# GNN plus top-2 mixture of experts on one core: translations of blocks into items moved behind the last runs, batch loads ahead of them

## The reference, cut to what matters

```python
x = x + gnn(layernorm(x), src, dst, edge_weight, W, b)
x = x + ffn(layernorm(x), gate_w, gate_b, W1, b1, W2, b2)

def gnn(f, src, dst, w, W, b):                 # 12500 nodes, 256 features, 212500 edges, dst sorted
    agg = segment_sum(f[src] * w[:, None], dst)
    return einsum('ni,oi->no', agg, W) + b

def ffn(x, ...):                               # 8 experts, 256 -> 512 -> 256
    probs = softmax(x @ gate_w + gate_b)
    top2_vals, top2_idx = top_k(probs, 2)      # each node goes to two experts
    out = sum over experts e of  cw[:, e] * (gelu(x @ W1[e] + b1[e]) @ W2[e] + b2[e])
```

## The kernel before, in words

| turn | items whose loads are issued | tiles translated | runs sent | batch (tiles) |
|---|---|---|---|---|
| 208 | 179, 180 | 72-75 | 92, 93 | |
| 209 | 181, 182 | 76-79 | 94, 95 | |
| 210 | 183, 184 | 80-83 | | 0 (48-51) |
| 211 | 185-187 | | 96, 97, then the tails | 1 (52, 53) |
| 212 | 188-190 | | | 2 (54-57) |
| 213 to 221 | three in each turn, to 216 | | | 3 to 9 in turns 213 to 219 |

## Time and profile before

### The profile page before, as it was taken

The page is one execution under the profiler, slowest core; times in us unless marked ns, Lnnn a source line. Parts: engine busy times, 40 slices in busy tenths (PEclk is TensorE's granted clock), DMA queues, the critical chain, the costliest instruction groups (busy, mean ns, idle before and its releaser), DMA issues.

```text
span 2566.9 us, 46927 instructions
## 1 busy us (share of the span) xinstructions
PE 2069.9 (81%) x11178; PEld 1625.8 (63%) x11179; DVE 1591.4 (62%) x6566; ACT 653.7 (25%) x1900; POOL 1802.5 (70%) x1909
## 2 busy tenths in 40 slices
PE   4666786688899889888897899896978878886595
PEld 2444564477677677765775678674757666765485
DVE  7888546446565465465666756776776656776344
ACT  3332111122222122221321223221223222232131
POOL 7665777777777777777767767577777777752473
PEclk8776888899999999998999999998989889998797
DMA  8766755867868879778788699597889788795696
GB/s 285 250 206 211 233 176 167 258 217 250 292 215 272 262 222 293 255 233 271 221 263 274 200 302 299 171 307 251 272 275 315 230 272 281 262 284 199 221 370 227
DMA packets 304350, 646.04 MB, mean 252 GB/s; under 512 B 62536, under 2 KB 197226, under 8 KB 291402
## 3 DMA queue, kind: packets, MB, share of 16 engines
q1 hardware_dynamic: 145320, 325.55, 37.4%
q0 software_dynamic: 90384, 248.17, 32.2%
q10 hardware_dynamic: 68370, 69.23, 7.7%
HBM read 543.70 MB, written 208.20 MB: 293 GB/s over the span
## 4 chain that ended last, share of the span: by engine, by line
POOL 26%; PE 19%; DVE 18%; issue 14%; DMA 11%; SPq 11%; ACT 1%; DVEq 1%; ACTq 0%; POOLq 0%
POOL rows L523 22%; SPq L504 8%; PE bank L885 7%; DMA slots<-stage 5%; PE bank L978 5%; PE bank L962 4%; DMA stage<-sorted_x 3%; POOL got L564 2%; DVE spread L1366 2%; DVE bn L1345 2%; SPq L454 1%; PE bank L905 1%; DVE pre_bn L1322 1%; DVE square_n L1413 1%; POOL rows L564 1%
## 5 line engine op out<-in xcount | busy, mean ns | idle before, releaser
L523 POOL DMA_INDIRECT rows<-xhat,src_t x1488 | 1423.0, 956 | 500.8 <-issue 446.2
L885 PE MATMUL bank<-rows,spread 128*80 128x256 f32 x3328 | 870.4, 421 | 163.4 <-DMA rows<-xhat,src_t 70.8
L885 PEld LDWEIGHTS bank<-rows,spread 128*80 128x80 f32 x3328 | 548.7, 168 | 445.7 <-issue 200.7
L978 PE MATMUL bank<-w,hT 128*128 x1736 | 439.1, 398 | 46.3 <-DVE y_sb L1593 29.0
L962 PEld LDWEIGHTS bank<-xiT,w 128*128 128x128 f32 x3472 | 423.9, 193 | 28.6 <-issue 8.2
L962 PE MATMUL bank<-xiT,w 128*128 128x128 f32 x3472 | 427.7, 277 | 9.8 <-ACT xiT L1150 5.6
L1166 ACT ACTIVATE hT<-bank,b1T 128x128 f32<-128x128 f32 x868 | 247.6, 368 | 672.7 <-PE bank L962 455.5
L978 PEld LDWEIGHTS bank<-w,hT 128*128 128x128 f32 x1736 | 326.8, 198 | 101.0 <-issue 61.7
L1379 DVE TENSOR_TENSOR acc<-acc,bank 128x160 f32 x208 | 66.9, 322 | 506.8 <-PE bank L875 455.7
L1366 DVE TENSOR_SCALAR spread<-iota_w,dst_rel,wgt 128x80 f32<-128x80 f32 x1488 | 366.2, 338 | 0.2
L523 POOL DMA_INDIRECT rows<-in_x,src_t x176 | 168.4, 957 | 75.9 <-issue 51.0
(11 more groups left out here) (191 smaller groups left out, 1893.3 us busy)
## 6 DMA issues: line engine op xcount, KB each, us to landing
w<-in_w SPq DMA_DIRECT2D x217, 512.0 KB
slots<-stage SPq DMA_DIRECT2D x760, 136.0 KB
xi<-slots SPq DMA_DIRECT2D x217, 136.0 KB
stage<-sorted_x ACTq DMA_DIRECT2D x98, 272.0 KB
rows<-xhat,src_t POOLq DMA_INDIRECT x1488
yq<-y_sb ACTq DMA_DIRECT2D x182, 128.0 KB
x_t<-in_x SPq DMA_DIRECT2D x97, 128.0 KB
x_d<-x_t ACTq DMA_DIRECT2D x97, 128.0 KB
```

Source lines behind the costliest of these rows:

```text
L523: pool.indirect_dma_start(rows[q][:, c, :], None, x if g < RAW else xhat, bass.IndirectOffsetOnAxis(ap=src_t[:, g * CG + c:g * CG + c + 1] ...
L885: done = nc.tensor.matmul(B_SUM[0:W, 0:D], spread[g % 2][:, c, :], rows[q][:, c, :], start=c == 0, stop=c == CG - 1)
L978: done = nc.tensor.matmul(bank[:, 0:D], hT[i % 2][:, j, :], w2[:, bass.ds(e, 1), j, :].rearrange("p o f -> p (o f)"), start=j == 0, stop=j ...
```

## The change

The planner and SP's `tail_turn` are changed. In the planner, `busy` stands for "this turn has a gather", `with_sums` for the usual plan (`not with_sums` is the plan for graphs of another shape, which these inputs don't take), and `sent_at` holds the parts whose last tile's runs have been given a turn; `NK - 1` is part 16, which is sent in turn 211.

```diff
-        while index_next < LATE and len(t.index) < (1 if busy else BATCH):
+        while index_next < LATE and len(t.index) < (1 if busy or not with_sums else 2 if NK - 1 in sent_at else 0):
...
-                for u in ([t.stage] if t.stage >= 0 else []) + t.quick:
-                    send(u)
+                if t.stage >= 0:
+                    send(t.stage)
                 if last_turns[0].batch >= 0:
                     store_batch(last_turns[0], first_batched)
                 else:
...
                     load_batch(plan, t, fast, first_batched)
                 for u in t.keeps:
                     load_kept(u)
+                for u in t.quick:
+                    send(u)
                 move_lists(t)
```

## The result

The kernel before took 2577.21 us in the median of its runs, the changed one 2560.94 us. The two medians differ by 16.3 us. The ratio of the runs on record is 0.9946, with a 95% interval from 0.9927 to 0.9965: faster by 0.54%, and the interval reaches to both sides of the 0.5% that the prediction took as its bound for no change. The forecast was 2563 us. The profiled executions took 2568.56 and 2557.23 us.

What follows compares the result with a forecast made beforehand. After the last gather, translations on the chain preparing the last tiles were taken to bound it, then full POOL, DMA and PE. Savings of 15.8 us less 1.2 added gave 14.6, from the 2578.02 median 2563.4 us; range 2550 to 2573.

Steps and rivals of the forecast that it cites:

- (a): Turn 208: four translations ahead of the last add_group leave the chain, 6.1 us less; ends 5.4 and 6.2.
- (b): SP: the store of tile 47 no longer stands ahead of the load of item 183's rows, 0.6 us less.
- (c): Turn 209: four translations taken away gain nothing, as DVE waited 3.63 us for PE there.
- (d): Turn 210: four translations ahead of list_items and the last part's place leave the chain, 6.1 us less.
- (e): PE before the last sort: shorter pause, down product at full clock, 1.8 us less; ends 0 and 1.9.
- (f): SP: two loads of batch 1 no longer stand between the last blank block and item 188's load, 1.2 us less.
- Turn 212: Two added translations ahead of list_items have no cover and delay turn 213's first result: 1.2 us more, at most 3.1.
- slow rival: From turn 212 on DVE sets the pace and PE's clock falls in five turns: 8.7 us more, 2587 us; chance 0.07.
- Turns 213 to 216: Two added translations in each turn are free; at most 3.1 us a turn, 12.5 us for the four.
- rival of the DMA engines: Full DMA engines hold the second stretch, up to about 2500 us: half the gain, 7.3 us, 2571 us; chance 0.11.
- more than forecast: PE's late pause and slow product near 2498 us also vanish: 4.3 us more gain, 18.9 less, 2559 us; chance 0.08.
- short gain: No clock return in (e), only 5.4 us in (a), 3.1 us lost in turn 212: 10.2 us less, 2568; chance 0.24.

Runs made afterwards that it cites:

- keep_208: The changed kernel, but four translations stay in turn 208 and the other eight go in pairs in turns 211 to 214: 2566.4 us, ratio to before 0.9957.
- sp_only: The kernel before with SP's new order alone, translations still four a turn in turns 208 to 210: 2570.0 us, ratio to before 0.9982.
- keep_209: The changed kernel, but four translations stay in turn 209 and the other eight go in pairs in turns 211 to 214: 2558.22 us, ratio to before 0.9936.
- keep_210: The changed kernel, but four translations stay in turn 210 and the other eight go in pairs in turns 211 to 214: 2568.89 us, ratio to before 0.9974.
- none_212_c: The changed kernel, but turn 211 translates four tiles and turn 212 none: 2559.78 us against 2579.13 of the kernel before, ratio 0.9915.
- busy_two_b: Repeat on a disturbed chip: the changed kernel, but all twelve translations in turns 196 to 207, two a turn: ratio 0.998 against 3451.88 us, inconclusive.

## Why the prediction was right, and where it was off

The mechanism was right in the first stretch and the time fell into the range, but one term was mis-sized threefold, and two of the signs that the prediction had named for being wrong did come: the last scatter moved by 3.7 us less than the load of item 188 (more than 3), and PE and POOL stood for DVE's results at the start of turn 213. Of the other signs, `add_group` came at 2315.15 us and item 188's rows at 2396.80, as forecast; item 183's rows came at 2350.34 instead of 2348.5, and the first result of turn 213 was 11.9 us earlier instead of 13.

In us behind the anchor, from the table above:

| step | forecast | measured |
|---|---|---|
| (a), (b): to item 183's rows | 6.7 | 5.3 |
| (c): turn 209 | 0 | nothing lost |
| (d), (e), (f): item 183's to item 188's rows | 9.1 | 10.8 |
| added translations: item 188's rows to the last scatter | -1.2 | -3.7 |
| last scatter to the end | 0 | -0.7 |
| together | 14.6 | 11.7 |

**(a) and (b)** came, and 1.9 us of them were lost again on the way. By its end the product of tile 96 had gained 6.6 us, as it took 1.03 us in place of 2.06, which answers the doubt about its clock; keep_208 gave 6.6 too. (b) adds 0.6, by sp_only. But the two halves of tile 94's sort took 1.27 us each, at a granted clock of 0.50, where before they took 0.73 and 0.91, which is 0.9 us that the sum did not have; PE had stood 3.58 us for rows ahead of them. In keep_209 and keep_210 the second half took 0.72 us, so this too differs from execution to execution. And tile 94's runs landed 1.06 us later. 6.6 + 0.6 - 0.9 - 1.1 is 5.2; measured were 5.3. The sort of before:

```profile
2336.65 0.73 PE L913 MATMUL bank<-xs,sort_mask 128*128 128x272 f32 x2 [2.01 <-DVE sort_mask L1532]
2337.87 0.91 PE L913 MATMUL bank<-xs,sort_mask 128*128 128x272 f32 x2 [0.49 <-ACT sorted_x L1123]
```

**(c)** was right: keep_209 isn't slower.

**(d) and (e)** were right in mechanism: the pause shrank from 7.05 to 1.57 us and the product from 3.78 to 1.99. keep_210 takes both back at once. (f) is the 1.3 us of sp_only. The three together brought 1.7 more than forecast, and this is not theirs: 0.9 is the landing of tile 96's runs, 4.21 us against 5.13, 0.2 the load of item 183's rows, 4.28 against 4.49, 0.4 the first down product behind these rows, 3.37 against 3.78, and 0.2 the sort of tile 96, which also ran at full clock.

**Turn 212 is the term that was mis-sized: -1.2 forecast, -3.7 measured.** That there was no cover behind that pair, how long DVE would be late, and that 1.3 us would come through to PE, was in the working. What was left out is that PE would then stand still, and for more than it was late. Before, PE waited 1.59 us for rows just ahead of that place and 0.59 us without a releaser in the profile (2431.29 and 2432.32 us); in the changed kernel the rows were there, so PE reached the place 2.1 us earlier behind item 188's load (its turning product at 2418.05 and at 2435.93: 21.25 us against 23.38), and stood for 4.22. The forecast priced the late result and not the clock that falls in the pause. That is 1.4 us on the down product (3.28 against 1.89) and 0.4 on the up product behind it (2.37 against 1.95). The slow rival had this very price, 1.8 us, and spread it over five turns; the likeliest case had it nowhere. With it the term would have been 1.2 + 1.8 = 3.0, and the stretch between the scatters of items 187 and 190 shows 3.0; but the parts are others, 1.7 for the wait and 1.3 for the down product, since the slow up product stands behind what item 190's result needs. That the sums agree is partly luck. none_212_c gives all of it back. Of the other 0.7 us, 0.5 came ahead of it: the scatter of item 187 stood 13.7 us behind the load instead of 13.2, since behind the long wait for the rows an up product took 2.91 us instead of 1.95. In none_212_c it stood 12.5 us behind. keep_208 to keep_210 and sp_only had 2.3 to 2.7 us for that product, with or without the pair, and before and none_212_c 1.95, so it was not the edit that made it.

The Trainium skill (TensorE: Matmul & The Clock Gate, What's actually happening) says that the array is throttled when it has been idle and that activity releases it. By that rule the fall behind 4.22 us of waiting is what one expects, and the trace agrees in the direction. How it goes in one case, the length of the pause alone doesn't say here: the down product took 1.99 us behind pauses of 1.57, 1.80 and, in the changed kernel, 2.59 us, but 2.81 behind 2.46 and 3.60 behind 2.64. What else decides was not found out.

**Turns 213 to 216** were free, as forecast. The lead of the scatters is 12.2 us at item 190 and 12.05 at the last, and none_212_c, with a pair in each of the four turns, took 128.7 us from item 188's load to the last scatter, where sp_only took 128.6 with none. (By 1.53 us for each tile the prediction's bound for the four turns is 12.2 us and not 12.5; nothing rests on it.) In 51 us of the full stretch the engines do as much as before (columns as in the earlier trace rows):

```profile
2430.00:2481.00 51.00, 49.37 (x341) 45.77 (x340) 35.34 (x120) 18.37 (x65) 38.82 (x40) 1.00 1.03 357
```

DVE has gone from 24.75 to 35.34 us of the 51, and POOL keeps its 38.8. So the rival in which DVE sets the pace in five turns has fallen: it does so in the one that the forecast named. The rival of the DMA engines has fallen too, as the lead did not shrink in proportion.

**POOL beside translations.** The casts at the ends of the two translations in turn 212 start at 2413.09 and 2414.65 us, and the gathers beside them took 0.96 and 0.95 us:

```profile
2413.06 0.96 POOL L564 DMA_INDIRECT got<-yq,gather_i  x1 [0.30 <-issue]
2414.33 0.95 POOL L564 DMA_INDIRECT got<-yq,gather_i  x1 [0.30 <-issue]
```

The one of 1.24 us stands beside combinations again, as in the earlier trace rows. The Trainium skill (SBUF — State Buffer, Who interferes with whom), by which such a cast locks GpSimd out, would have made these gathers longer by up to 0.18 us; here the measurement shows nothing of it, and the 0 of the forecast stands.

What the traces do show is DVE waiting for POOL. Two of DVE's short instructions in `list_items` took 0.40 and 0.44 us, and the list 5.83 us instead of 5.60:

```profile
2414.86 0.40 DVE L1544 CAST up_i<-queue_end 1x8 int32<-1x8 f32 x1
...
2416.07 0.44 DVE L1550 TENSOR_SCALAR upto_n<-upto_n 1x8 f32<-1x8 f32 x1
```

The first began 0.53 us into the gather of 2414.33 us and ended with it (2415.26 and 2415.28 us). The second did the same with the next one (2416.51 and 2416.53 us):

```profile
2415.58 0.95 POOL L564 DMA_INDIRECT got<-yq,gather_i  x1 [0.30 <-issue]
```

All four kernels with a pair in turn 212 have the two at 0.40 to 0.45 us, the three without have them at 0.22 to 0.23. From 2395 us on, 36 of the casts and tensor_scalars in the seven traces took 0.08 to 0.25 us more than the shortest of their kind. All 36 began 0.46 to 0.64 us into an indirect DMA of POOL and ended with it or, with 128x256 elements, 0.1 us behind it. Not all that begin there are held, and why a gather holds DVE in its second half only was not looked into. In turn 212 it costs 0.2 us.

The late pause is still there, 2.59 us at 2489.29 in place of 2.46, but with its product at 1.99 us. So of the 4.3 us that the rival "more than forecast" asked for about 0.8 came, without a trace of it in the last scatter's lead, and not by the edit: keep_208 and keep_210 had 3.48 us behind 2.70 and 3.78 behind 3.02 at this place, sp_only 1.99 behind 2.67.

Behind the last scatter 0.7 us were lost; 0.5 of it is the landing of that scatter, 3.63 us against 3.12.

**The time itself.** The forecast of 2563.0 us was taken from the median, which lies some 9 us above the profiled execution, and that was the better base: the traces' 11.7 us from 2577.21 would give 2565.5, 14.6 would give 2562.6, and measured were 2560.94. The measured ratio is too wide to tell these apart. By the traces the gain lies below the 13 to 16.5 us of the forecast's own case and nearer to that of the short gain, 10.2; that the median came within 2 us of 2563 is in part luck. The anchor shows why the runs scatter: it lies between 2312.11 and 2329.16 us in the seven profiled executions, a range of 17 us in a part that no version changes, while what follows it can be compared to one or two us.

## What to carry to other kernels

Work that has cover in one turn may have none in the next: before moving it, find for every turn what the engine's first result is waited for by, and put the work where the engine itself waits (here turn 211, ahead of a wait of 19 us, and not turn 212). Where a wait reaches TensorE, its price is the wait *and* the products that run below full clock behind it; here 1.7 and 1.3 to 1.6 us. Taking a wait away brings both back, as before the last sort. And count from a common event instead of from the start of the program: it made differences of 2 us readable in executions that began the stretch up to 17 us apart.

The version with the pair moved out of turn 212 has the shortest tail of all, 4.6 us less than the changed kernel. Its ratio to before, 0.9915 [0.9885, 0.9945], and that of the changed kernel, 0.9946 [0.9927, 0.9965], overlap, and they come from different comparisons: that it is the faster one is shown by the trace and not by the times.

## What was not expected of the hardware

Equal DMAs in the same place differ by more than some of the edits: tile 94's runs landed in 4.72 to 7.27 us in the seven executions. On the disturbed chips every version took 3437 to 3516 us in the median. The page of busy_two_b shows PE busy for 2308.6 instead of 2073.3 us, with a mean granted clock of 0.83 instead of 0.91, but POOL as busy as ever (busy us, share of the span, instructions):

```profile
PE 2308.6 (67%) x11178; PEld 1771.9 (52%) x11179; DVE 1584.2 (46%) x6566; ACT 666.1 (19%) x1900; POOL 1801.0 (53%) x1909
```

What POOL waited for in that whole execution:

```profile
POOL rows L523 <- PE bank L887: 704.3, 94, 15.1
POOL rows L523 <- issue: 452.2, 1470, 1.3
POOL rows L523 <- remote: 209.9, 91, 3.8
```

POOL's gathers waited 704 us for that product of PE there, and 46.7 us in the changed kernel. The lower clock and the longer waits go together there; what held those chips back was not found out.
